# Two lasting places for keys and values, and sixteen gather places at the end of the first mixture, in a two-layer transformer step on one core

## What is computed

```python
x = x + L0_xattn(layernorm(x), ctx)      # one head, masked
x = x + L0_attn(layernorm(x))            # gated delta rule with convolutions
x = x + L0_ffn(layernorm(x))             # 8 experts, the best 2 of each row
x = x + L1_xattn(layernorm(x), ctx)      # 16 heads
x = x + L1_attn(layernorm(x))            # 16 query heads, 4 key heads, rotary
x = x + L1_ffn(layernorm(x))             # 16 experts, the best 4, and a shared one
```

```python
k = ctx[b] @ Wk.T + bk       # 257 x 256 for each of the 64 batches
v = ctx[b] @ Wv.T
```

## Time and profile before

| what | us |
|---|---|
| median of 3 runs | 1781.69 |
| profiled execution, time | 1793.83 |
| profiled execution, span | 1792.0 |
| PE busy | 1591.9 (89%) |
| DVE busy | 1211.0 (68%) |
| ACT busy | 788.2 (44%) |
| POOL busy | 613.7 (34%) |
| mean DMA rate | 120 GB/s |

### The profile page before, as it was taken

One profiled execution on the slowest core, in us unless ns is written; L12 is line 12 of the kernel. 1 busy time (PEld: TensorE's weight loads), 2 busy tenths in 40 slices (PEclk: granted clock), 3 DMA queues, 4 the chain that ended last, 5 costly groups with the idle time before them and its releaser, 6 DMA issues. The chain is left out here.

```text
span 1792.0 us, 41190 instructions
## 1 busy us (share of the span) xinstructions
PE 1591.9 (89%) x16490; PEld 1215.2 (68%) x16490; DVE 1211.0 (68%) x2401; ACT 788.2 (44%) x1856; POOL 613.7 (34%) x526
## 2 busy tenths in 40 slices
PE   5986888999988959999999498999989879999998
PEld 3443366555675759999997374566668768689997
DVE  4577889680077448888881316677759867677888
ACT  1222642121133324344442234788827722476664
POOL 2330300000020066666643303587528745203210
PEclk8997989999899969999999798999989979999999
DMA  9990059401043555555538771555500000001001
GB/s 292 321 322 12 1 179 214 128 13 30 2 141 89 153 193 210 204 199 210 193 132 195 188 229 60 184 166 161 168 25 1 1 27 17 13 1 42 24 7 48
DMA packets 143213, 214.84 MB, mean 120 GB/s; under 512 B 38128, under 2 KB 116528, under 8 KB 137136
## 3 DMA queue, kind: packets, MB, share of 16 engines
q1 hardware_dynamic: 106848, 104.06, 20.2%
q0 software_dynamic: 10368, 58.47, 9.8%
q10 hardware_dynamic: 25808, 49.68, 9.5%
HBM read 164.91 MB, written 47.25 MB: 118 GB/s over the span
## 5 line engine op out<-in xcount | busy, mean ns | idle before, releaser
L286 PE MATMUL ps<-kv_ctx,kv_w 128*128 128x257 f32 x512 | 133.1, 396 | 43.2 <-PEq L1824 19.3
L2000 DVE TENSOR_TENSOR f_hL<-f_hr,f_hH 128x512 fp32r<-128x512 f32 x92 | 135.4, 1526 | 46.8 <-ACT f_hH L1951 46.7
L2158 POOL TENSOR_TENSOR a_pr<-a_pr,a_inv 128x1028 f32<-128x1028 f32 x64 | 121.6, 1900 | 72.8 <-DVE a_inv L2278 72.5
L286 PEld LDWEIGHTS ps<-kv_ctx,kv_w 128*128 128x128 f32 x512 | 94.4, 195 | 64.7 <-issue 33.9
L290 PE MATMUL ps<-kv_w,kv_ctx 128*128 128x256 f32 x512 | 124.8, 387 | 13.8 <-ACT b_kv L310 9.3
L96 PE MATMUL ps<-f_xTH,f_w1H 128*128 128x256 f32 x368 | 108.0, 293 | 18.9 <-issue 18.2
L2248 ACT ACTIVATE a_pr<-ps,a_neg 128x257 f32<-128x257 f32 x256 | 117.7, 477 | 2.6 <-DVE a_neg L2298 2.6
L290 PEld LDWEIGHTS ps<-kv_w,kv_ctx 128*128 128x128 f32 x512 | 95.1, 192 | 32.4 <-ACT b_kv L310 13.9
L1512 POOL TENSOR_TENSOR b0m_pm<-b_dr,b_gates 128x256 f32<-128x256 f32 x16 | 13.2, 830 | 296.5 <-SPq L1477 270.1
L97 PE MATMUL ps<-f_xTL,f_w1H 128*128 128x256 f32 x368 | 106.0, 288 | 0.0
L98 PE MATMUL ps<-f_xTH,f_w1L 128*128 128x256 f32 x368 | 105.9, 288 | 0.0
(11 more groups left out here) (421 smaller groups left out, 4532.0 us busy)
## 6 DMA issues: line engine op xcount, KB each, us to landing
a_kv<-kv SPq DMA_DIRECT2D x64, 513.0 KB, 3.6
a_ctxT<-in_ctxT SPq DMA_DIRECT2D x32, 514.0 KB, 7.8
a_ctxR<-in_ctx SPq DMA_DIRECT2D x32, 512.0 KB
kv<-b_kv ACTq DMA_DIRECT2D x31, 513.0 KB, 5.7
kv_ctx<-in_ctxT ACTq DMA_DIRECT2D x61, 257.0 KB, 4.0
kv<-f_raw ACTq DMA_DIRECT2D x15, 513.0 KB, 11.3
outs<-f_yo SPq DMA_DIRECT2D x23, 256.0 KB, 2.1
kv<-f0r_kv ACTq DMA_DIRECT2D x9, 513.0 KB
```

The source lines that it names most:

```text
L286: done = e.matmul(out[:, 0:NK], self.w[:, 0, c, cols(part)], ctx[:, c, :], start=(c == 0), stop=(c == DC - 1))
L2000: e.tensor_tensor(h[1][:, j % 2, 2 * q:2 * q + 2, :], hr[:, q, :, :], h[0][:, j % 2, 2 * q:2 * q + 2, :].bitcast(F32), ALU.subtract).then_ ...
L2158: e.tensor_tensor(pr[:, b % 3, :, :], pr[:, b % 3, :, :], inv[:, b % 2, :].unsqueeze(2).to_broadcast([P, HG, NK]), ALU.mult).then_inc(*p_p ...
```

## The change

Two places of keys and values now belong to `KeysAhead` and live as long as it does (`KeysAhead.own`), in SBUF at the other end. A `KvPlace` counts its own stores and waits for the last one only when it is written again. The host layers name the places they use, the lasting ones among them: `delta_attention` those two, routing and queries those two and one of their own, the first mixture's tail two in `raw1`, those two and the routing's own, five in all. A layer's end waits only for the places that the layer owns; `A.end` is gone.

The first mixture's tail takes 14 contexts and the query block 10 (15 and 9 before). ACT copies 36 of the 42 parts before the norm's square root and 6 behind it (`TAIL`). The gathers have 16 places, two for each of 8 tiles, in the whole of `raw2`. `xr` moves into the routing block's own memory; for that the wait for the stores of its rows stands ahead of the first gather of weights.

```diff
-AHEAD = (31, 9, 15, 9)
+AHEAD = (31, 9, 14, 10)
+class KvPlace:
+    def __init__(self, Y, at, name):
+        self.at, self.st, self.used = at, Y.sig("dma", name), 0
+    def free(self, e):
+        if self.used:
+            e.wait_ge(*self.st.at(16 * self.used))
+    def store(self, e, out):
+        e.dma_start(out, self.at).then_inc(*self.st.up(16))
+        self.used += 1
 class KeysAhead:
+        self.own = [KvPlace(Y, at, f"kv{n}") for n, at in enumerate(places(Y.sb("kv", [P, 2, KV])))]
...
-            if part == 0 and own >= len(self.kv):
-                e.wait_ge(*self.st[s].at(16 * (own // len(self.kv))))
+            if part == 0:
+                place.free(e)
...
-    def end(self, e):
-        many, count = len(self.kv), (self.last - self.first) // 3
-        for s in range(many):
-            e.wait_ge(*self.st[s].at(16 * ((count - s + many - 1) // many)))
 def delta_attention(K):
-        A.host(Y, AHEAD[0], (6, 7), places(sb("kv", [P, 2, KV])))
+        A.host(AHEAD[0], (6, 7), A.own)
 def delta_mix(K, ahead, F, dr, gates, wo, nw):
                 K.norms["f0"].act(e)
-                ahead.end(e)
 def experts_0(K):
-        xr = sb("xr", [P, NT, D])
+        kv1 = KvPlace(Y, sb("kv1", [P, KV])[:, :], "kv1")
...
+            xr = Z.sb("xr", [P, NT, D])
...
-            A.host(Z, AHEAD[1], (6, 7), places(Z.sb("kv", [P, 3, KV])))
+            A.host(AHEAD[1], (6, 7), A.own + [kv1])
...
                     A.act(e, 3 * AHEAD[1])
-                    A.end(e)
...
-        A.host(Y, AHEAD[2], (0, 1, 2, 3), places(place1[:, 0:3 * KV].rearrange("p (s n) -> p s n", s=3)))
-        yg = place2[:, 0:4 * D].rearrange("p (s n) -> p s n", s=4)
+        kv2, kv3 = (KvPlace(Y, at, f"kv{n + 2}") for n, at in enumerate(
+            places(place1[:, 0:2 * KV].rearrange("p (s n) -> p s n", s=2))))
+        A.host(AHEAD[2], (0, 1, 2, 3), [kv2, kv3] + A.own + [kv1])
+        yg = place2.rearrange("p (t k n) -> p t k n", k=2, n=D)
...
+                e.wait_ge(*st_r.at(16 * NT))
                 gather1(0)
-                e.wait_ge(*st_r.at(16 * NT))
...
-                for n in range(2 * NT):
-                    if n >= 4:
-                        e.wait_ge(*v_x.at(n - 3))
-                    t, k = n // 2, n % 2
-                    e.indirect_dma_start(yg[:, n % 4, :], None, K.outs, bass.IndirectOffsetOnAxis(
-                        slot[:, k * NT + t:k * NT + t + 1], 0)).then_inc(*ld_g[n % 4].up(16))
+                for t in range(NT):
+                    if t >= RING:
+                        e.wait_ge(*v_x.at(2 * (t - RING) + 2))
+                    for k in range(2):
+                        e.indirect_dma_start(yg[:, t % RING, k, :], None, K.outs, bass.IndirectOffsetOnAxis(
+                            slot[:, k * NT + t:k * NT + t + 1], 0)).then_inc(*ld_g[t % RING].up(16))
...
-                A.act(e, 3 * AHEAD[2])
+                A.act(e, 3 * AHEAD[2] - TAIL)
                 K.norms["a1"].act(e)
-                A.end(e)
+                A.act(e, TAIL)
+                for place in (kv1, kv2, kv3):
+                    place.free(e)
...
 def cross_attention_1(K):
-            A.host(Z, AHEAD[3], (6, 7), places(Z.sb("kv", [P, 3, KV])))
+            kv1 = KvPlace(Z, Z.sb("kv1", [P, KV])[:, :], "kv1")
+            A.host(AHEAD[3], (6, 7), A.own + [kv1])
...
-                    A.end(e)
+                    for place in A.own + [kv1]:
+                        place.free(e)
```

More of the change, by code:

```diff
@@ L252, in __init__, with host, host_of @@
         self.mm, self.ev = Y.sig("pe", "kv"), Y.sig("act", "kv")
[L253 to L259, removed]
+        self.own = [KvPlace(Y, at, f"kv{n}") for n, at in enumerate(places(Y.sb("kv", [P, 2, KV])))]
+        self.formed = self.taken = self.last = 0
+        self.hosts = []
+    def host(self, count, banks, kv):
+        self.hosts.append((self.last, banks, kv))
+        self.last += 3 * count
+    def host_of(self, j):
+        return [h for h in self.hosts if h[0] <= j][-1]
     def load(self, e, b):
@@ L275, in pe @@
             b, part = divmod(j, 3)
-            s, many = b % self.SLOTS, len(self.banks)
-            ctx, out = self.ctx[s], self.K.ps[:, self.banks[(j - self.first) % many], :]
+            first, banks, _ = self.host_of(j)
+            s, many = b % self.SLOTS, len(banks)
+            ctx, out = self.ctx[s], self.K.ps[:, banks[(j - first) % many], :]
             if j == 0:
@@ L302, in act @@
             b, part = divmod(j, 3)
-            own = b - self.first // 3
-            s = own % len(self.kv)
-            kv, src = self.kv[s], self.K.ps[:, self.banks[(j - self.first) % len(self.banks)], :]
+            first, banks, kv = self.host_of(j)
+            place = kv[(b - first // 3) % len(kv)]
+            src = self.K.ps[:, banks[(j - first) % len(banks)], :]
             e.wait_ge(*self.mm.at(j + 1))
-            if part == 0 and own >= len(self.kv):
-                e.wait_ge(*self.st[s].at(16 * (own // len(self.kv))))
+            if part == 0:
+                place.free(e)
             if part < 2:
-                done = e.activation(kv[:, cols(part, NK)], src[:, 0:NK], ACT.Identity, bias=self.bk[:, part:part + 1])
+                done = e.activation(place.at[:, cols(part, NK)], src[:, 0:NK], ACT.Identity, bias=self.bk[:, part:part + 1])
             else:
-                done = e.activation(kv[:, 2 * NK:KV], src, ACT.Copy)
+                done = e.activation(place.at[:, 2 * NK:KV], src, ACT.Copy)
             done.then_inc(*self.ev.up())
@@ L318, in act @@
                 e.wait_ge(*self.ev.at(j + 1))
-                e.dma_start(self.K.kv[b], kv).then_inc(*self.st[s].up(16))
-    def end(self, e):
-        many, count = len(self.kv), (self.last - self.first) // 3
-        for s in range(many):
-            e.wait_ge(*self.st[s].at(16 * ((count - s + many - 1) // many)))
+                place.store(e, self.K.kv[b])
 def places(t):
@@ L1807, in experts_0 @@
         ld_w1, ld_w2 = ([Y.sig("pooldma", f"{n}{s}") for s in range(2)] for n in ("w1", "w2"))
-        ld_g = [Y.sig("pooldma", f"g{s}") for s in range(4)]
+        ld_g = [Y.sig("pooldma", f"g{s}") for s in range(RING)]
         st_y = [Y.sig("dma", f"y{s}") for s in range(2)]
```

22 lines of the change are left out of this document (11 added, 11 removed).

## The result

The changed kernel takes **1788.97 us** (median of 20 executions, 1781.55 to 1800.61), the kernel before 1782.88 beside it: ratio 1.005, 95% interval 1.0032 to 1.0067. It is slower by half a per cent, and 16.8 us above the forecast of 1772.2. The profiled execution has a span of 1798.8 us (before: 1792.0).

A forecast was written before the change was run, and what follows sets the result against it. PE was busy 89%; the first mixture's end was taken as DMA-bound, then held by gather latency. Routing end -1.2, mixture end -9.9 and query layer +1.6 gave -9.5, from 1781.69 to 1772.2 us; range 1764 to 1780.

The forecast's parts named there:

- Sixteen places for gathers: First mixture's end: DMA stays full until its owed work is done, so the norm ends at 1011.0, 15.8 us earlier.
- a share below 0.9 between 950 and 1005: Sign in the first mixture's tail that the sum of DMA work is not what bounds the kernel.
- the term of 0.67 and 3.19 us of engine time: First mixture's tail: DMA engine time per gather, 0.67 us, and per context of keys, 3.19 us.
- the debt of 59.7 us: DMA work owed until the last gather lands: 21.4 us for 32 gathers plus 38.3 us for twelve contexts.
- first rival: First mixture: gathers get more of the DMA engines, data in at 991; sum -16.1, 1765.6 us; chance 0.22.
- Six parts behind the norm: First mixture's end: two contexts' key and value parts now follow the norm and lengthen the layer, +6.0 us.
- a wait that the prediction called free: First mixture's end: waits for the two borrowed places cost nothing, their last stores being issued before the norm.
- The routing layer's end: End of the routing layer no longer waits for the last store, -1.2 us, bounds 0 and 1.9.
- The tenth context in the query layer: Query layer: one more context, +3.46 us, less 1.86 as PE comes without a long pause; net +1.6 us.
- The second rival: Query layer: ACT waits for stores left in flight, first copy 6 us late; +5.5 us, 1777.7; chance 0.15.
- if these land in 6 us, nobody waits: Query layer's start: the two lasting places' stores, issued 4 and 0.4 us before the previous layer's end, delay nobody.
- The slower rival: First mixture: norm comes no earlier but six parts still follow it; +6.4 us, 1788.1; chance 0.07.

The follow-up runs named there:

- e4: Changed kernel with eight gather places instead of sixteen, on chip A; ratio 0.9948 to the kernel before, 1770.99 us beside 1779.52.
- e3: Changed kernel with no parts of keys behind the norm (TAIL 0), on chip A; ratio 0.994, 1770.06 us beside 1779.52.
- e16: Changed kernel with later gathers in groups of four, four POOL fills of 128x512 behind each group, on chip B; one run, 1772.2 us.
- e1: Changed kernel with the four gather places and gather loops of the kernel before, on chip A; ratio 1.002.
- e5: Changed kernel run again unaltered, on chip B; ratio 1.0059 to the kernel before.
- e6: Changed kernel with eight gather places and no parts of keys behind the norm, on chip B; ratio 1.0074.
- e8: Changed kernel run again unaltered, on chip C; ratio 1.0046 to the kernel before.
- e10: Changed kernel with eight gather places, the six parts kept behind the norm, on chip C; ratio 0.9984.
- e12: Changed kernel with a short POOL fill of 128x32 after each gather, on chip D; ratio 1.0029.
- e14: Changed kernel with a POOL fill of 128x512 between gathers and no parts behind the norm, on chip D; ratio 0.9938.
- e15: Changed kernel unaltered, as the control on chip D; one run, 1803.94 us.
- e2: Kernel before with sixteen gather places and nothing else of the change, on chip A; ratio 0.9971.
- e11: Changed kernel with a POOL fill of 128x512 after each gather, six parts kept behind the norm, on chip C; ratio 0.9979.
- e18: The kernel of e14 (fills of 128x512 between gathers, no parts behind the norm) a second time, on chip B; ratio 0.9936.
- e9: The kernel of e3 (changed kernel, no parts behind the norm) again, on chip C; ratio 1.0045.
- e13: Changed kernel with contexts 42 to 53 loaded and stored in only 8 columns, removing most keys' DMA there; one run, 1817.04 us.
- the spaced kernels: Changed kernel with a POOL fill of 128x512 between gathers, with six parts behind the norm (e11, 0.9979) or none (e14, 0.9938; e18, 0.9936).

## Why the prediction was wrong

**The step that failed** is the one headed "Sixteen places for gathers": "So I go by work that must be done, not by shares ... From 949.5, at a share of 1.01". It took for granted that the DMA engines stay full until the last gather, which needs ACT to go on copying and issuing. The last sentence of the prediction named the sign, a share below 0.9 between 950 and 1005. The share fell to 0.68, 0.63 and 0.32. The engines had too little to do because ACT issued almost nothing, since PE's signals reached it late: it began a copy 5.7 to 10.8 us after the last one though the part had long been ready. In the profiled execution the mixture came to +3.0 us, not -9.9; the routing layer (-1.5, forecast -1.2) and the query layer (+2.6, forecast +1.6) are close, so the mixture is 12.9 of the 13.6 us by which the sum was off there. Counted from the experts' first gather of weights, the norm ended 4.2 us earlier than before, not 15.8.

**Where there is no pause the sum was too cautious.** It had the norm end 62.2 us after the first gather (1011.0 - 948.8). In e4 it is 998.42 - 943.86 = 54.6 us, in e3 and e16 some 57.5, in e3 with fourteen contexts ahead of it and not twelve. What failed is the term of 0.67 and 3.19 us of engine time, taken as constants: in the earlier trace rows full DMA engines (1.01) move 232 GB/s, in e3's window above they move 270 at the same share (1.02). And the gathers' share did not stay at the quarter of the earlier trace rows. The DMA view of e3 from 950 to 985:

```profile
q10 hardware_dynamic: 3205, 6.15, 57.1%
q0 software_dynamic: 1307, 3.58, 46.3%
...
f_raw<-outs,f_slot POOLq DMA_INDIRECT x26, 8.5
```

With more gathers in flight they took 46.3% of the engines, and each still landed in 8.5 us. The two rows give 0.59 us of engine time a gather (46.3% of 35 us for 3.58 MB, and a gather is 0.13 MB) and 2.56 us a context (57.1% for 6.15 MB, at 0.79 MB each). With these the debt of 59.7 us is 49.6, an estimate from one stretch. So the first rival's mechanism was true where nothing paused: e3's statistics are done at 990.86, 49.0 us after its first gather, where the rival had the data in after 42. Against it stood the rule of the Trainium skill, "DMA: Bandwidth & Descriptors", section "Queues, rings and completion order", that an engine takes turns between the rows packet by packet, from which I had inferred that a longer row gets no more turns, with the earlier trace rows as support. This run doesn't bear out the use I made of it: a queue that its places hold to four says little of what a fuller one gets. The rival was priced at 1765.6. Its best case here, e3, took 1770.06 beside 1779.52.

**Six parts behind the norm, +6.0**: right where it was without a pause, 6.5 us from the root in e4 and about 7 in e1. In the changed kernel they came to 1025.83 - 1017.62 = 8.2 us, and 2.1 of these are a wait that the prediction called free, for the borrowed places. ACT issued its last store at 1022.90 and then waited until 1025.3 for a store of a borrowed place that it had issued at 1015.97, just ahead of the root: issued before the norm doesn't mean landed. The same wait took 1 to 5 us in e5, e6, e8 to e10, e12, e14 and e15, and nothing in the others with five places. ACT's timeline:

```profile
1015.97 0.33 ACTq L249 DMA_DIRECT2D kv<-f_raw  x1
...
1022.90 0.33 ACTq L249 DMA_DIRECT2D kv<-kv_kv  x1
```

**The routing layer's end, -1.2**: right in this pair, by more than its wait explains. DVE's last is at 625.09, POOL's first gather at 626.17; the gap of 628.24 to 630.72 in the earlier trace rows has shrunk from 2.48 to 1.08 us, and the layer by 1.5. The gap is 1.08 in every kernel with the change's routing; in e2, which has the routing of before, it is 1.85. The layer itself varies more: from -2.0 to +0.4 us in the kernels with the change's routing, +0.3 in e2.

**The tenth context in the query layer, +1.6**: too low. The layer was longer by 2.6 us in the changed kernel, and by 0.3 to 7.6 over all those with ten contexts and five places. The second rival's wait is there: 6.22 us at the first copy, where 6 us late was its estimate. It is there in e3 as well (9.3 us in three waits, the longest 3.9). The claim "if these land in 6 us, nobody waits" had no row, and the row there was, 12.4 us, spoke against it.

**The slower rival** gave 1788.1, and 1788.97 was measured, but not for its reason, so that is luck; its own sign, a norm that ends after 1020.5, did not show (1018.12). It had the gathers themselves bound and the norm no earlier; the gathers were issued 36 us sooner, and what was late was the chain from PE over ACT to the root. What it got right is the bill: little gained at the norm, six parts and the tenth context to pay.

**A size behind all of it.** The forecast took its 9.5 us from one execution of the kernel before that was 12 us above the median. In e3 the three layers together are 15.0 us shorter than in it (routing +0.4, mixture -19.7, query +4.3), but e3's median is 9.5 us below; in e4 it is 19.9 against 8.5 (routing -1.9), in e2 8.8 against 5.8 (routing +0.3), and in e1 the layers are 2.7 shorter (routing -0.5) and the median 4.5 longer. So that execution was probably long in just these layers, by 3 to 11 us on chip A, and a gain read from it is too large. A second profile of the kernel before, which would show it, was not taken.

## What to carry to other kernels

An engine freed of its waits may issue faster than anything did before in the kernel; before counting the gain, ask what else on the chip has only been seen beside the slow rate. Here a filler of half a microsecond between two indirect DMAs turned 0.5% slower into no slower on one chip (e8 and e11, 1.0046 and 0.9979); with the tail gone as well it was 0.6% faster (e14, e18), where the unspaced kernel without a tail, on another chip, was 0.5% slower (e9). Where an instruction that others wait for (the root) stands behind a long list of unrelated work on its engine, any delay of that work moves it: freeing the gathers moves the wait, it doesn't remove it. And when two kernels differ in a way that the code doesn't explain, run both again together before building a theory on it; e3 and e9 are one program, 0.6% faster on one chip and 0.5% slower on another.

## What the runs showed of the hardware

- With POOL's indirect DMAs 1.27 to 1.32 us apart in a run of 32, PE's signals to ACT came late: parts lay ready for up to 33 us, in its midst 5.7 to 15.7 us passed between two of ACT's copies, and PE got 6 to 10 us of work done in 30. ACT's signals to PE were not late (0.15 us at most in the changed kernel). ACT's idle time began 10.4 to 12.6 us after the first gather. It was so in every profile of such a kernel on chips B, C and D (e5, e6, e8, e9, e12, e13, e15) and in neither on chip A (e2, e3, at 1.26 and 1.27). At 1.41 us apart it was there in a weaker form in e10 and not in e4, at 1.66 us and above in none.
- It needs no crowded DMA: with the keys' queue at 0.9% and the gathers at 38.9% it was the same, with some three gathers in flight.
- The engines' own code isn't what is late. From 950 to 990 the changed kernel fetches one packet of it, and e16, which has no pause, also one. The DMA view of the changed kernel:

```profile
q8 instruction: 1, 0.02, 0.2%
```

- The records show that the semaphore goes up late, not why; that signals between engines share something with what POOL writes for each gather is a guess. Nor is it known what sets chip A apart, or how long a run at the high rate must be (twenty passed in e16).
- A DMA share of 1.0 is no fixed rate: full engines moved 217 GB/s from 960 to 990 in the kernel before, and 239 to 279 in e1 to e4 and the spaced kernels.
